# Fetching a stage's spectra and images one stage earlier, and cosine and sine sums in the gelu stage's transforms

## What is computed

```python
p = _fno_layer(av, Pcw, Psw, H, W)
a = _inorm(p + xa, attn_w, attn_b)
an = _inorm(a, norm2_w, norm2_b)
m = _fno_layer(an, m0cw, m0sw, H, W, inner_norm=True, act=True)    # gelu
m = _fno_layer(m, m1cw, m1sw, H, W, inner_norm=True, act=False)
out = _inorm(m, mon_w, mon_b) + a
```

## Time and profile before

| | |
|---|---|
| median of 3 runs | 1094.45 us (1094.44 to 1097.9) |
| profiled execution, own time | 1093.65 us |
| its span | 1092.0 us |
| PE busy | 810.1 us (74%) |
| DVE busy | 682.0 us (62%) |
| ACT busy | 405.7 us (37%) |
| POOL busy | 365.4 us (33%) |
| mean granted TensorE clock | 0.892 of full |

### The profile page before, as it was taken

How to read it: one execution, slowest core, us unless ns; L and a number is a source line. 1 busy time by engine, 2 the same in 40 slices (tenths; PEclk the granted TensorE clock), 3 DMA queues, 4 the chain that set the end, 5 groups by cost and what they waited for, 6 DMA issues and landing times. The chain is left out here.

```text
span 1092.0 us, 36677 instructions
## 1 busy us (share of the span) xinstructions
PE 810.1 (74%) x16050; PEld 586.8 (54%) x16050; DVE 682.0 (62%) x1427; ACT 405.7 (37%) x882; POOL 365.4 (33%) x262
## 2 busy tenths in 40 slices
PE   0498493789999846999922899568767777776797
PEld 0365231222222216777712799457766666666686
DVE  4797597578888784555548899744444444443132
ACT  0297341123222263555533466423333333332121
POOL 0022471689999800111100000324444444442000
PEclk9999697699999967999965999888888888888899
DMA  9566710576464303334120776489999999998587
GB/s 363 113 186 153 163 27 3 185 292 196 165 198 168 108 0 95 95 83 141 49 90 7 192 192 191 106 191 252 270 266 264 264 263 264 263 264 188 156 261 212
DMA packets 270430, 189.36 MB, mean 173 GB/s; under 512 B 29108, under 2 KB 259221, under 8 KB 269269
## 3 DMA queue, kind: packets, MB, share of 16 engines
q1 hardware_dynamic: 189811, 131.47, 44.5%
q10 hardware_dynamic: 75426, 44.17, 16.6%
q0 software_dynamic: 5120, 12.75, 4.3%
HBM read 154.45 MB, written 33.07 MB: 172 GB/s over the span
## 5 line engine op out<-in xcount | busy, mean ns | idle before, releaser
L1960 PE MATMUL po<-pa,room 128*32 128x16 f32 x8320 | 146.8, 221 | 84.7 <-DMA room<-_L_conv_weight_imag_dram 59.3
L1960 PEld LDWEIGHTS po<-pa,room 128*32 128x32 f32 x8320 | 144.3, 162 | 92.5 <-issue 69.0
L979 POOL TENSOR_TENSOR q<-wb,xb 128x1536 f32<-128x1536 f32 (+1 forms) x51 | 170.2, 3364 | 41.0 <-DMA wb<-wv 33.3
L1049 DVE TENSOR_TENSOR q<-pw,xb 128x1536 f32<-128x1536 f32 (+1 forms) x85 | 140.7, 1702 | 25.0 <-PE acc L1019 13.7
L1019 PE MATMUL acc<-q,pt 128*32 128x384 f32 (+1 forms) x1088 | 103.7, 494 | 15.8 <-DVE q L1049 15.7
L2101 DVE TENSOR_TENSOR osl<-po,neg 128x128 f32<-128x128 f32 x64 | 18.3, 286 | 149.9 <-ACT neg L2034 149.9
L1913 POOL DMA_DIRECT2D os_<-osl x64 | 45.4, 713 | 182.7 <-DVE osl L2112 174.8
L1903 POOL COPY cols<-y 128x512 f32<-128x512 f32 x32 | 38.3, 1196 | 152.4 <-POOLq L1667 146.7
L2034 ACT ACTIVATE neg<-po 128x272 f32<-128x272 f32 x32 | 12.7, 397 | 197.0 <-issue 182.1
L1947 PE MATMUL px<-wbat,cols 128*32 128x130 f32 x2176 | 76.3, 292 | 4.2 <-DVE wbat L2072 3.0
L1019 PEld LDWEIGHTS acc<-q,pt 128*32 128x32 f32 x1088 | 27.7, 110 | 90.7 <-issue 55.1
(11 more groups left out here) (326 smaller groups left out, 1578.4 us busy)
## 6 DMA issues: line engine op xcount, KB each, us to landing
room<-_L_conv_weight_real_dram ACTq DMA_DIRECT2D x32, 520.0 KB, 9.7
room<-_L_conv_weight_imag_dram ACTq DMA_DIRECT2D x32, 520.0 KB, 12.7
room<-_L_conv_weight_real_dram SPq DMA_DIRECT2D x32, 520.0 KB, 7.0
room<-_L_conv_weight_imag_dram SPq DMA_DIRECT2D x32, 520.0 KB, 10.3
xb<-xns SPq DMA_DIRECT2D x64, 192.0 KB, 3.1
wb<-wv SPq DMA_DIRECT2D x16, 576.0 KB, 5.9
yall<-in_x_dram SPq DMA_DIRECT2D x4, 2048.0 KB, 14.6
xd<-in_x_dram SPq DMA_DIRECT2D x16, 512.0 KB, 4.2
```

Source lines behind the costliest of these rows:

```text
L979: nc.gpsimd.tensor_tensor(q2[:, t % 2, :, :, 0:m], bc(weights(blk, n), 2, NB), spectra(blk), ALU.mult).then_inc(s_qp, 1)
L1049: V.tensor_tensor(q1[:, t % 2, :, :, 0:m], bc(pw[t % 4][:, 0:3 * m].rearrange("p (r m) -> p r m", r=3), 2, NB), spectra(blk), ALU.mult).th ...
L1960: e = nc.tensor.matmul(po[u][32 * g:32 * g + 32, 512 * q + 16 * m:512 * q + 16 * m + 16], wsl[u][:, :, q * KWF + KWF - 1 - kw], xsl[u][:, ...
```

## The change

Three things are done.

1. In stage 5 the forward transform along h is by cosine and sine sums. `forward_h` multiplies by the matrix `ph` (33 cosine and 32 sine columns) and not by `fh` (128 columns: real and imaginary part of 64 frequencies). `forward_w` is one matmul for the sine part (`fw2`, 256 columns, into `pq`) and one for the cosine part (`fw1`, 264 columns, into `pw`), and no longer two accumulating matmuls of 512. ACT copies the cosine and the sine part of `forward_h` apart (`even`, `odd`) and has a new step `sines_copy`, which brings `pq` to SBUF; it is placed after gelu and square of the next group. `copy_out` on DVE becomes a copy and two two-operand instructions (sum and difference of the two parts), and waits for `sines_copy`.
2. Loads are issued earlier: the first four groups' `mg` in stage 4; the spectra `yt` batch by batch (32 partitions each) in stage 5 as soon as a batch has been stored, so that the last one alone is issued at the end of stage 5; `qh` and the first pair of images of stage 7 in stage 6. The second layer's weights are issued after the second batch of `mg`.
3. For this the tiles `qh`, `cols`, `mg5` and `yt` are allocated earlier, and the first pair of stage 7 lies in `cols`.

```diff
+    c["ph"] = np.concatenate([np.cos(tp), -np.sin(tp[:, 1:])], 1) / 128
...
+            @block.sync                      # stage 4
+            def _(sp):
+                for u in range(GPB):
+                    sp.dma_start(mg5[:, u], mixr[:, u * GI:u * GI + GI, :]).then_inc(s_mg5[u], 16)
...
             @block.sync                      # stage 5
             def _(sp):
+                sp.dma_start(ph[:, :], c["ph"]).then_inc(s_ph, 16)
...
-                each_batch(load)
+                def hidden_back(b):
+                    for q in s_yo:
+                        sp.wait_ge(q, 16 * (b + 1))
+                    sp.dma_start(yt[32 * b:32 * b + 32].rearrange("p w r h -> p (w r h)"), ys[32 * b:32 * b + 32].rearrange("i m k -> i (m k)")).then_inc(s_yt, 16)
+                load(1)
                 sp.dma_start(room[:, 2 * M2:4 * M2], bass.AP(mpl.tensor, 2 * M2, [[0, 128], [1, 2 * M2]])).then_inc(s_m1, 16)
+                load(2)
+                hidden_back(0)
+                load(3)
+                for b in range(1, NB):
+                    hidden_back(b)
...
                     for i in range(GI):
-                        m = nc.tensor.matmul(pf[:, 128 * i:128 * i + 128], yall[:, g * GI + i, :], fh[:, :], start=True, stop=True)
+                        m = nc.tensor.matmul(pf[:, 128 * i:128 * i + 65], yall[:, g * GI + i, :], ph[:, :], start=True, stop=True)
...
-                    for r, f in enumerate((fw1, fw2)):
-                        m = nc.tensor.matmul(pw[:, :], f[:, :], yf[:, u % 2, r].rearrange("w i k -> w (i k)"), start=(r == 0), stop=(r == 1))
-                    m.then_inc(s_f2, 1)
+                    nc.tensor.matmul(pq[0:2 * KW, 0:32 * GI], fw2[:, :], odd[:, u % 2].rearrange("w i k -> w (i k)"), start=True, stop=True).then_inc(s_f3, 1)
+                    nc.tensor.matmul(pw[:, 0:33 * GI], fw1[:, :], even[:, u % 2].rearrange("w i k -> w (i k)"), start=True, stop=True).then_inc(s_f2, 1)
...
                 pe.wait_ge(s_pz, 1)
+                pe.wait_ge(s_ph, 16)
...
-                    act.activation(yf[:, u % 2], pf[:, :].rearrange("w (i r k) -> w r i k", i=GI, r=2), ACT.Copy).then_inc(s_e1, 1)
+                    act.activation(even[:, u % 2], v[:, :, 0:33], ACT.Copy)
+                    act.activation(odd[:, u % 2], v[:, :, 33:65], ACT.Copy).then_inc(s_e1, 1)
+                def sines_copy(b, u):
+                    g = GPB * b + u
+                    act.wait_ge(s_f3, g + 1)
+                    wait(act, s_e2, g - 1)
+                    act.activation(sines[:, u % 2], pq[0:2 * KW, 0:32 * GI].rearrange("m (i k) -> m i k", i=GI), ACT.Copy).then_inc(s_sn, 1)
...
                         lagged(b, u, 0, gelu)
+                        lagged(b, u, 1, sines_copy)
...
-                    V.tensor_copy(yo[:, u], pw[:, :].rearrange("m (i k) -> m i k", i=GI)).then_inc(s_e2, 1)
+                    dve.wait_ge(s_sn, g + 1)
+                    P, Q = pw[:, 0:33 * GI].rearrange("m (i k) -> m i k", i=GI), sines[:, u % 2]
+                    V.tensor_copy(yo[:, u, :, 0:1], P[:, :, 0:1])
+                    V.tensor_tensor(yo[:, u, :, 1:32], P[:, :, 1:32], Q[:, :, 0:31], ALU.add)
+                    V.tensor_tensor(yo[:, u, :, 63:31:-1], P[:, :, 1:33], Q, ALU.subtract).then_inc(s_e2, 1)
...
             @block.sync                      # stage 6
             def _(sp):
-                for g, (lo, hi) in enumerate(COLS):
-                    sp.dma_start(yt[:, lo:hi].rearrange("p w r h -> p (w r h)"), ys[:, 2 * lo:2 * hi, :].rearrange("i m k -> i (m k)")).then_inc(s_ld[g], 16)
+                sp.dma_start(qh[:, :], c["qh"]).then_inc(s_qh, 16)
+                for v, src in enumerate((mixd, x)):
+                    sp.dma_start(pair0[:, v], src[0:GI].rearrange("i h w -> h i w")).then_inc(s_mg7[0], 16)
...
-                    dve.wait_ge(s_ld[g], 16)
+                    if g == 0:
+                        dve.wait_ge(s_yt, 16 * NB)
...
             @block.sync                      # stage 7
             def _(sp):
-                sp.dma_start(qh[:, :], c["qh"]).then_inc(s_qh, 16)
                 def load(b, u):
                     g = GPB * b + u
+                    if g == 0:
+                        return
                     wait(sp, s_q7, g - 1)
```

More of the change, by code:

```diff
@@ L1059, in build @@
         c1b, c2b = (fac.enter_context(nc.sbuf_tensor(n, [128, NI], F32)) for n in ("c1b", "c2b"))
+        qh = fac.enter_context(nc.sbuf_tensor("qh", [128, 128], F32))
+        cols = fac.enter_context(nc.sbuf_tensor("cols", [128, 2, 4, 2, NI], F32))
+        pair0 = cols[:, :, :, :, :].rearrange("p u q s i -> p (u q s i)").rearrange("p (v i w) -> p v i w", v=2, i=GI)
+        ahead = ExitStack()
+        mg5 = ahead.enter_context(nc.sbuf_tensor("mg5", [128, GPB, GI, WW], F32))
+        mixr = mixd.rearrange("i h w -> h i w")
         DC = (slice(None), 0, 0, slice(0, 1))
@@ L1347, in inverse_w @@
             m.then_inc(s_s2, 1)
+        yt = ahead.enter_context(nc.sbuf_tensor("yt6", [128, KW, 2, KH], F32))
+        s_yt = sem("hidden_columns_loaded")
+        s_qh, s_mg7 = sem("p7_matrix_loaded"), sems("p7_images_loaded", 2)
         with ExitStack() as p5:
@@ L1362, in build @@
             sq = sb("sq5", [128, 2, GI, WW])
-            yf = sb("yf5", [128, 2, 2, GI, KH])
+            even = sb("even5", [128, 2, GI, 33])
+            odd = sb("odd5", [128, 2, GI, 32])
+            sines = sb("sines5", [2 * KW, 2, GI, 32])
+            ph = sb("ph5", [128, 65])
             yo = sb("yo5", [2 * KW, GPB, GI, KH])
@@ L1470, in body @@
                         lagged(b, u, 0, gelu)
+                        lagged(b, u, 1, sines_copy)
                 each_batch(body)
                 forward_copy(NB - 1, GPB - 1)
+                sines_copy(NB - 1, GPB - 1)
             @block.vector
@@ L1672, in pb @@
                 return p7.enter_context(nc.psum_tensor(name, shape, F32))
-            mg, xg = (spare[:, v * 2 * GI * WW:(v + 1) * 2 * GI * WW].rearrange("p (u i w) -> p u i w", u=2, i=GI) for v in range(2))
+            pair1 = spare.rearrange("p (v i w) -> p v i w", v=2, i=GI)
+            mg, xg = ((pair0[:, v], pair1[:, v]) for v in range(2))
             ts = sb("ts7", [128, 2, KW, GI])
             zs = sb("zs7", [128, 2, GI, 128])
-            qh = sb("qh", [128, 128])
             pz = pb("pz7", [128, GI * 128])
@@ L1776, in hidden @@
                         k = g * GI + i
-                        m = V.scalar_tensor_tensor(mg[:, u % 2, i], mg[:, u % 2, i], c2b[:, k:k + 1], xg[:, u % 2, i], ALU.mult, ALU.add)
+                        m = V.scalar_tensor_tensor(mg[u % 2][:, i], mg[u % 2][:, i], c2b[:, k:k + 1], xg[u % 2][:, i], ALU.mult, ALU.add)
                     m.then_inc(s_m7, 1)
@@ L1781, in hidden @@
                         k = g * GI + i
-                        m = V.scalar_tensor_tensor(y[:, i], y[:, i], c1b[:, k:k + 1], mg[:, u % 2, i], ALU.mult, ALU.add)
+                        m = V.scalar_tensor_tensor(y[:, i], y[:, i], c1b[:, k:k + 1], mg[u % 2][:, i], ALU.mult, ALU.add)
                     m.then_inc(s_q7, 1)
```

24 lines of the change are left out of this document (13 added, 11 removed).

## The result

The changed kernel takes 1081.11 us (median of 4 runs, 1077.31 to 1082.24), the kernel before, beside it, 1096.18 us (4 runs, 1094.44 to 1098.76): ratio 0.986, 95% interval 0.983 to 0.989. A second time on another chip it took 1081.15 us (6 runs) for 1096.28, ratio 0.987 (0.984 to 0.989). The prediction of 1081.4 us was right, and the transforms and both kinds of fetch each gained where they were expected to, though four smaller terms were wrong: the start and the end of stage 5, the seam to stage 6, and stage 6 itself. That the time is met to 0.3 us is partly luck, as shown further down.

A forecast was written before the change was run, and what follows sets the result against it. PE was taken to bound the gelu stage, DMA the seams. Terms -1.0 + 8.1 + 1.0 + 1.7 + 3.2 = 13.0 us off 1093.65, plus 0.8 for the median: 1081.4 us, own range 1077.5 to 1084.5, wider range 1076.5 to 1089.8.

The forecast's parts named there:

- PE's saving: Each stage 5 step: `forward_w` saves 0.85 us, `forward_h` nothing since weight loads set its pace; PE's work 7.39 to 6.54.
- What takes PE's place: Stage 5 steps: ACT's loop and DVE's chain through `sines_copy` tie at 6.81 us; 14 steps gain 8.1 us.
- X: Time of `copy_out`'s three instructions on DVE in stage 5, put at 0.8 us; DVE's chain is 6.02 + X.
- Start of stage 5: PE waits for `ph`, starts 0.56 us later, and more work meets the low clock: first `add` about 1.0 us later.
- End of stage 5: Last `add` to last store: about 7.45 us instead of 8.48, 1.0 us gained.
- Seam to stage 6: Last store to first product: last quarter of `yt` issued without the stage's end, 8.7 us for 10.39, 1.7 gained.
- Seam to stage 7: Start of stage 7: `qh` and first images already there, DVE's wait replaced by PE's work, 3.2 us gained (1.2 to 4.5).
- The transforms gain nothing: Rival, stage 5: the ACT, DVE, ACT hand-over lasts 7.39 us; only 4.9 us gained, 1089.5 us; chance 0.15.
- the early transfers aren't worth it: Rival, seams to stages 6 and 7: 1.7 and 2.6 us of the gains are lost, 1085.7 us; chance 0.08.
- PE stays the bound: Rival, stage 5: PE sets steps of 6.5 us, late `sines_copy` hides better; 4.3 us more gained, 1077.1; chance 0.08.
- Slower: Rival, stage 5: from X = 1.75 DVE's chain eats all other gains; at X = 2.3, 1102.5 us; chance 0.03.
- The clock falls: Rival, stage 5: PE's waits of 0.3 us a step lower the clock, PE's 6.5 become 12.5, about 1161 us; chance 0.02.

The follow-up runs named there:

- square_late: Changed kernel with ACT's square moved behind the next group's `rows_back`, same work; 1075.59 us in one run, steps 6.550 us.
- square_late_wide: `square_late` with `forward_h` back at 128 columns, 63 of them zeros whose products nobody reads; 1074.46 us in one run.
- after: The profiled execution of the changed kernel, no further edit; own time 1081.58 us, against 1093.65 us for the kernel before.
- copy_twice: Changed kernel with two more two-operand instructions in `copy_out` on DVE, into a tile nobody reads; 1094.26 us in one run.
- busy_stage6: Changed kernel with the square after the next `rows_back`, `ph` loaded in stage 4, and 22 unread matmuls added on PE in stage 6; 1083.41 us.
- busy_stage6_short: `busy_stage6` with 10 added multiplications instead of 22; 1076.52 us (5 runs), ratio 0.9836 to the kernel before.
- after_again: The changed kernel with no edit, timed again on another chip; 1081.15 us (6 runs), ratio 0.987 to the kernel before.
- the halves: Kernel before with part 1 alone, 1089.51 us, ratio 0.9943; and with parts 2 and 3 alone, 1088.2 us, ratio 0.9944.
- images_not_ahead: Changed kernel with stage 7's first pair of images loaded in stage 7, `qh` still ahead; 1086.98 us in one run.
- transforms_only: Kernel before with part 1 of the change alone, all loads where they were; 1089.51 us, ratio 0.9943 to the kernel before.

## Why the prediction was right, and where it wasn't

- **The total.** The parts touched gained 13.8 us in the profiled pair (14.2 less the 0.4 behind `forward_h(0)`), 13.0 predicted. By the medians the gain is 15.1 us both times. The forecast of 1081.4 was counted from 1094.45 us, the median of three runs, while more runs of the kernel before gave 1095.05 to 1096.28 us: a gain forecast too small and a start counted too low cancel, and within the gain the seams' misses cancel in part. That much of the 0.3 us is luck.
- **PE's saving.** 0.85 us a step from `forward_w`, none from `forward_h`, 6.54 us in all: right, 6.55 where nothing else binds (`square_late`), and none from `forward_h` to the last digit (`square_late_wide`). The earlier trace rows were weaker ground than the prediction made of them: it set two loads at 41.99 us beside two at the granted clock 0.50, and at 41.99 the profile reads 1.00, with no clock event on record before 49.65. `square_late_wide` shows the point, not those rows.
- **What takes PE's place.** Right in mechanism and size: 6.81 predicted, 6.78 measured; both loops within 0.1 us, DVE's just ahead, ACT's by its pieces. X = 0.8 was 0.78: reversed writes and rows of 31 elements cost what plain ones cost. The link `sines_copy` to `copy_out` took 0.46 for 0.41, and each of DVE's hand-overs in the chain 1.13 for 1.14.
- **Start of stage 5.** Wrong in sign: 1.0 lost predicted, 0.5 gained. PE does wait for `ph`, and starts 1.69 us after SP's first instruction instead of 1.26: 0.43 later, 0.56 forecast (0.4 to 0.8 over the eight profiles in which it waits). But the term took the low stretch from 428.6 to 435.3 as fixed, and that step failed. In after it ended at 433.2, so that `inverse_w(0)` took 2.05 us and not 3.78. That the wait shortens it was only seen and not tested: where PE waits for `ph` it was 3.4 us in six profiles, 6.8 in one and 10.2 in `copy_twice`; where it doesn't, 6.8 in four (`busy_stage6` among them) and none in `busy_stage6_short`.
- **End of stage 5.** Mis-sized: 1.0 predicted, 0.23. The working holds at full clock (7.45 predicted, 7.47 in `square_late_wide`). In after the clock fell between `forward_h` and `forward_w` of the last group, and the two matmuls took twice as long. PE had waited 1.59 us for gelu and then 0.75 for `odd` (0.68 and 1.11 at the same places before). Before, the clock fell 10 us after the last `add`, behind the stage's work. That the longer wait brought it forward wasn't tested.
- **Seam to stage 6.** 1.7 predicted, 2.20: the parts were 3.26 us for the store to land and 4.93 for the load, not 3.4 and 5.3; L374's landings were a little long a stand-in. What the prediction calls the load of all of `yt` was, for the first product, its first DMA alone. The two fetches for stage 7 on the same queue, behind it, hide as said.
- **Stage 6** was put at nothing without a reason, and lost 0.38: its transposes begin at the low clock in either kernel, and the stretch to DVE's first instruction of stage 7 is 33.6 to 35.0 us among the profiles without added work; it is short where the clock rises early (583.4 in `after_again`, 586.8 in after).
- **Seam to stage 7.** 3.2 predicted, 3.12, and DVE's addition waits for PE as said. But the two agree partly by luck, since the clock was low for 3.4 us in both profiles: the same kernel gave 4.6 in `after_again`, outside the 4.5 that stood as the upper bound.
- **The rivals.** "The transforms gain nothing" and "the early transfers aren't worth it" are refuted by the halves. "PE stays the bound" is false for this order on ACT and true for `square_late`. "Slower" needed an X of over 1.7, and X was 0.78. "The clock falls" showed only in `copy_twice`, at 0.4 us each time.

What decides for how long the clock stays low at a seam is left open. The runs show only that it varies with no edit. Loading `ph` earlier was tried only together with the square's move.

## What to carry to other kernels

Before costing a saving on the bounding engine, close the loops that pass through the others and compare their lengths: here 0.85 us off PE became 0.61, and moving one instruction that only the sum of squares waits for (the square) out of the chain gave back 0.23 of the remaining 0.24. A transfer whose producer ends just before its consumer starts is worth splitting by producer, so that the last piece can be issued before the stage's end: of the 2.2 us here, 1.8 came from that. A seam's price depends on the clock it happens to get, by up to 4 us here, so a term taken from one profile's low stretch needs a range of its own.

## What the runs showed of the hardware

- Sixteen passes with their own 128x128 float32 weights take 2.00 us with 65 moving columns and 2.05 with 128, at full clock.
- The granted clock at a stage's start differs between executions of one kernel: from none to 3.4 us low in stage 7 of the changed kernel, which moves `forward_h(0)` from 7.99 to 9.51 us. With 10.2 us low it was 12.17 in a kernel with all fetches in place.
- In `copy_twice`, where PE waits some 0.9 us in each step of 7.43, the granted clock fell to 0.50 twice in 14 steps, and rose again each time after 3.4 us. With 0.2 us in 6.78 it didn't fall between the `add`s, in any of the four profiles with these steps (after, `after_again`, `images_not_ahead`, `transforms_only`).
- After 9.6 us of idling PE worked 3.5 us at the low clock until the full one was granted (`busy_stage6`), and 2.8 us in `busy_stage6_short`.
- Two-operand instructions of DVE with a reversed output (256 elements) took 0.42 us, and with rows of 31 elements (248) 0.40 us: as much as plain ones of this size by the estimate from the earlier trace rows.
